# Expert loop of an attention and mixture-of-experts kernel: the second bias of odd tiles added in PSUM, GpSimd's additions one iteration later, the routing operations in the even tiles

## The reference, cut to what matters

```python
x = x + xattn(layernorm(x), ctx_768, ...)     # 8192 tokens of 512, 16 heads, FFN 1024
# then the mixture of experts, one expert per token:
logits = xt @ Wg.T;  top1 = argmax(logits)    # 8 experts
xhat = (xt - mean) * rsqrt(var + 1e-5)
for e in range(8):                            # H = 128
    h = gelu((xhat * s_e + b_e) @ w1_e + b1_e)
    y = y + (top1 == e) * (h @ w2_e + b2_e)
x = x + y
```

## Time and profile before

| | |
|---|---|
| median of 3 runs | 1581.79 us (1581.66 to 1583.35) |
| the profiled execution | 1584.45 us, span in the trace 1582.6 us |
| PE busy | 1515.4 us, 96% |
| DVE busy | 1037.9 us, 66% |
| POOL busy | 441.9 us, 28% |
| expert loop in the trace | first product of B_Y at 1402.79 us, last tile's L1506 at 1577.9 us |

### The profile page before, as it was taken

One profiled execution on the slowest core, in us unless ns is written; L12 is line 12 of the kernel. 1 busy time (PEld: TensorE's weight loads), 2 busy tenths in 40 slices (PEclk: granted clock), 3 DMA queues, 4 the chain that ended last, 5 costly groups with the idle time before them and its releaser, 6 DMA issues.

```text
span 1582.6 us, 24339 instructions
## 1 busy us (share of the span) xinstructions
PE 1515.4 (96%) x7988; PEld 1254.6 (79%) x7988; DVE 1037.9 (66%) x2496; ACT 713.1 (45%) x2015; POOL 441.9 (28%) x312
## 2 busy tenths in 40 slices
PE   6799999999999999999999999999999999997998
PEld 3688788787878787878787788878787878776886
DVE  5756566675758576766666675757575757467776
ACT  2545445353535363635444353535353636333443
POOL 3422122121222222212131122122222222136776
PEclk8899999999999999999999999999999999999999
DMA  9200101112020202020101101010101011548773
GB/s 230 80 28 1 54 1 40 42 31 74 3 86 1 74 14 74 22 75 21 61 27 54 34 23 38 17 54 1 54 1 54 1 54 54 215 153 261 232 226 112
DMA packets 67736, 105.93 MB, mean 67 GB/s; under 512 B 26967, under 2 KB 35432, under 8 KB 66591
## 3 DMA queue, kind: packets, MB, share of 16 engines
q1 hardware_dynamic: 56814, 70.68, 15.9%
q0 software_dynamic: 10800, 33.70, 5.5%
HBM read 59.47 MB, written 46.72 MB: 67 GB/s over the span
## 4 chain that ended last, share of the span: by engine, by line
PE 60%; DVE 23%; DMA 7%; ACT 4%; issue 3%; POOL 2%; DVEq 0%; POOLq 0%; SPq 0%; ACTq 0%
PE bank L1025 13%; PE bank L1050 12%; PE bank L887 11%; PE bank L911 5%; PE bank L1005 5%; DMA region<-rows,pos 4%; DVE actH L994 4%; PE bank L1455 4%; PE bank L1499 4%; DMA rows<-in_x 3%; DVE xn L845 2%; POOL region L1193 2%; ACT actH L988 2%; PE bank L1119 2%; PE bank L1438 2%
## 5 line engine op out<-in xcount | busy, mean ns | idle before, releaser
L1050 PE MATMUL bank<-w,actH 128*128 128x512 f32 x1536 | 373.8, 393 | 4.6 <-DVE actH L1040 4.6
L1025 PE MATMUL bank<-actA,w 128*128 128x512 f32 x1536 | 366.7, 394 | 0.0
L1025 PEld LDWEIGHTS bank<-actA,w 128*128 128x128 f32 x1536 | 286.0, 188 | 62.2
L1050 PEld LDWEIGHTS bank<-w,actH 128*128 128x128 f32 x1536 | 282.4, 188 | 62.9 <-DVE actH L1040 8.6
L970 POOL TENSOR_TENSOR E<-E,rc 128x1232 f32<-128x1232 f32 x64 | 145.0, 2265 | 447.6 <-DVE rc L965 447.6
L1040 DVE TENSOR_TENSOR actH<-htmp,actH 128x512 fp32r<-128x512 f32 x128 | 88.7, 693 | 166.8 <-ACT actH L1036 148.1
L1035 ACT ACTIVATE htmp<-bank,b 128x512 f32<-128x512 f32 x128 | 88.2, 689 | 226.1 <-PE bank L1025 217.4
L887 PE MATMUL bank<-actA,wq 128*128 128x512 f32 x768 | 182.0, 390 | 0.0
L943 ACT ACTIVATE E<-bank,mx 128x77 f32<-128x77 f32 x512 | 157.6, 365 | 45.4 <-DVE mx L920 45.4
L887 PEld LDWEIGHTS bank<-actA,wq 128*128 128x128 f32 x768 | 144.2, 188 | 30.4 <-issue 0.5
L1193 POOL DMA_INDIRECT region<-rows,pos x64 | 63.1, 985 | 373.0 <-DVE pos L1187 333.9
(11 more groups left out here) (165 smaller groups left out, 2063.3 us busy)
## 6 DMA issues: line engine op xcount, KB each, us to landing
rowB<-region SPq DMA_DIRECT2D x71, 258.0 KB
rows<-in_x SPq DMA_DIRECT2D x64, 256.0 KB, 3.5
e_raw<-in_E SPq DMA_DIRECT2D x16, 256.0 KB, 2.7
region<-padrow SPq DMA_DIRECT2D x9, 258.0 KB, 2.6
w_raw<-in_W SPq DMA_DIRECT2D x1, 2048.0 KB, 10.3
w_raw<-in_W SPq DMA_DIRECT2D x2, 1024.0 KB, 8.5
e_parts<-e_high SPq DMA_DIRECT2D x8, 256.0 KB, 2.0
e_parts<-e_low SPq DMA_DIRECT2D x8, 256.0 KB, 2.3
```

Of the source, the lines that this page charges most:

```text
L1025: mm = pe.matmul(p[:], w, a, start=k == 0 and j == 0, stop=k == KD - 1 and j == 2)
L1050: mm = pe.matmul(p[:], a, w, start=m == 0 and j == 0, stop=m == MF - 1 and j == 2)
```

## The change

Four edits, all in the expert loop:

1. Odd tiles: DVE no longer adds b2 to the row in SBUF. In B_Y(t) it adds b2 to the product in PSUM (`p = p + b2`, one input and the output in PSUM), then does L1488(t+1), and in a new step B_ROW(t) adds PSUM and row as before (`dve_bout`). Even tiles keep POOL's addition and one operation in B_Y.
2. POOL's addition of an even tile is in a step of its own, B_B2, three tiles ahead and not four: it stands in odd iterations, behind the scatter of an odd tile.
3. The drips of the loop move to even iterations: two after B_ROW and one after B_H, so three in two iterations in place of four.
4. SCAT of block 15 moves from iteration 6 to 14, TABLE2 from 8 to 5, PAD(e) from 10 + 2e to 16 + 2e. Registers: NREG 4 to 8.

```diff
-                3: [("RK", NBLK - 1)], 5: [("COUNT", 1)], 6: [("SCAT", NBLK - 1)], 8: [("TABLE2",)]}
-        LATE.update({10 + 2 * e: [("PAD", e)] for e in range(NE)})
+                3: [("RK", NBLK - 1)], 5: [("COUNT", 1), ("TABLE2",)], 14: [("SCAT", NBLK - 1)]}
+        LATE.update({16 + 2 * e: [("PAD", e)] for e in range(NE)})
         for t in range(-5, NT):
-            for kind, ahead in (("B_Y", 0), ("B_G", 1), ("B_X", 5), ("B_XT", 4), ("B_H", 3)):
+
+            for kind, ahead in (("B_Y", 0), ("B_G", 1), ("B_ROW", 0), ("B_X", 5), ("B_B2", 3), ("B_XT", 4), ("B_H", 3)):
                 if 0 <= t + ahead < NT:
                     step(kind, t + ahead)
+                if kind in ("B_ROW", "B_H") and t % 2 == 0:
+                    step("DRIP", 2 if kind == "B_ROW" else 1)
...
-        DRIP = {"KP": 5, "Q": 2, "PT": 2, "AV": 2, "HLO": 12, "Y": 1, "TT": 1, "B_Y": 1, "B_H": 1}
+        DRIP = {"KP": 5, "Q": 2, "PT": 2, "AV": 2, "HLO": 12, "Y": 1, "TT": 1}
...
-        NREG = 4
+        NREG = 8
...
-        def add_b2(eng, who, t):
-
-            eng.wait_ge(S["b_xT"], t + 1)
-            if t < 2:
-                eng.wait_ge(L["eb"], 32)
+        def pool_b2(pool, t):
+
+            if t % 2:
+                return
+            pool.wait_ge(S["b_xT"], t + 1)
+            if t == 0:
+                pool.wait_ge(L["eb"], 32)
             r = rowB[t % NROW][:, 0:D]
-            eng.tensor_tensor(r, r, pick(b2e, expert(eng, who, t)), ALU.add).then_inc(b_xb[t % 2], 1)
-
-        def pool_bx(pool, t):
-            if t % 2 == 0:
-                add_b2(pool, "pool", t)
-
-        def dve_b2(dve, t):
-            if t % 2:
-                add_b2(dve, "dve", t)
+            nc.gpsimd.tensor_tensor(r, r, pick(b2e, expert(pool, "pool", t)), ALU.add).then_inc(S["b_rb"], 1)
...
         def dve_by(dve, t):
             dve.wait_ge(S["b_y"], t + 1)
-            dve.wait_ge(b_xb[t % 2], t // 2 + 1)
+            p = of("B_Y", t)
+            if t % 2:
+                dve.tensor_tensor(p[:], p[:], pick(b2e, expert(dve, "dve", t)), ALU.add).then_inc(S["b_pb"], 1)
+            else:
+                dve.wait_ge(S["b_rb"], t // 2 + 1)
+                dve_bout(dve, t)
+
+        def dve_brow(dve, t):
+            if t % 2:
+                dve.wait_ge(S["b_pb"], t // 2 + 1)
+                dve_bout(dve, t)
+
+        def dve_bout(dve, t):
             r = rowB[t % NROW][:, 0:D]
             dve.tensor_tensor(r, of("B_Y", t)[:], r, ALU.add).then_inc(S["b_out"], 1)
...
-            "B_XT": {"pe": pe_bx, "act": act_bx, "dve": dve_b2, "pool": pool_bx},
+            "B_XT": {"pe": pe_bx, "act": act_bx},
+            "B_B2": {"pool": pool_b2},
+            "B_ROW": {"dve": dve_brow},
```

More of the change, by code:

```diff
@@ L264, in xattn_moe_kernel @@
             "pe_cnt dve_cnt dve_pad dve_tab dve_e1a pe_e1 dve_e1 act_e2 dve_e2 "
-            "b_xT b_xTs b_h b_hb b_gl b_g b_ghi b_glo b_y b_out").split()}
+            "b_xT b_xTs b_h b_hb b_gl b_g b_ghi b_glo b_y b_rb b_pb b_out").split()}
         pe_k, pe_v = S["pe_k"], S["pe_v"]
-        b_xb = [sem("b_xb0"), sem("b_xb1")]
         sched = []
```

## The result

The changed kernel takes 1588.23 us (median of 6 runs, 1587.24 to 1591.57) against 1581.72 us (1580.41 to 1583.35) in the same series: ratio 1.0044, interval 1.0031 to 1.0056. It is 6.5 us slower; 9.4 us faster was forecast. The profiled execution took 1587.24 us, its span is 1585.4 us. A second profiled run of each (e1, e12) gives 1583.7 and 1586.9.

What follows compares the result with a forecast made beforehand. PE was taken to nearly bound tiles 21 to 69, with more lost before. Terms of -5.0 (tiles 21 to 69), -4.7 (5 to 21) and +0.3 (0 to 5) sum to -9.4: 1581.8 to 1572.4 us, range 1566 to 1580.

Steps and rivals of the forecast that it cites:

- Part 4: Tiles 5 to 21: scatters at 14; together with Part 3 the loss falls from 12.7 to 8.0 us, -4.7 us.
- the stop: Iterations 9 to 11: L1466's unexplained 2.91 us wait, counted as gone; might return at SCAT for about 3.5 us.
- Rival (b): Expert loop: the stop returns at SCAT, or drips stall in iterations 16 to 20 too; 1576 us, chance 0.18.
- three signs of being wrong: Profile after: PSUM addition longer than 0.72 us, steady pairs waiting on POOL's L1424, or no stretched drips.
- Part 3: Even iterations 6 to 14: the first drip stalls at POOL's addition, 1.0 us a pair, 5.0 us in all.
- Tiles 0 to 5: Start of the expert loop: one more row-statistics stall, +1.0, less 0.7 us from DVE's emptier queue: +0.3 us.
- forecast wait of L1506(18) for POOL: Tile 18, behind the scatters: L1506 waits 2.4 us for POOL's addition, and PE waits behind it.
- Part 1: Tiles 21 to 69: PSUM addition takes 0.69 us, even tiles are on time, 0.21 us in 24 pairs: -5.0 us.
- rival (e): Odd tiles: the PSUM addition is long, 3.5 us per 0.1 us beyond 0.72, up to 1590 us; chance 0.08.
- Part 2: POOL's queue: 4.05 us of work fits a pair's 4.30; the addition keeps 1.7 us of slack, before 4.8.
- rival (d): Even tiles wait for POOL, whose pair takes 4.51 us; the 5.0 us gain goes, 1577.4 to 1580 us; chance 0.11.
- Rival (c): Drips: only one starting inside POOL's addition waits, 2.25 us in place of 5.0; 1569.6 or 1568 us; chance 0.13.

Runs made afterwards that it cites:

- e1: The kernel before, unchanged, once more for a second trace: a single execution of 1585.53 us beside a median of 1584.86 us in its series.
- e12: The kernel after, unchanged, once more: 1589.51 us, 1.0045 of the kernel before.
- e8: The kernel after with its three drips behind `hb` of odd tiles in place of even ones: 1583.64 us, 1.0019 of the kernel before.
- e15: The kernel after with the four scatters back in iteration 6, PAD and TABLE2 as after: 1.0028 of the kernel before.
- e17: The kernel before with only the LATE table of after (scatters at 14, TABLE2 at 5, PAD from 16 on): 1.0015 of the kernel before.
- e5: The kernel after with SCAT, TABLE2 and PAD where they were before: 1589.1 us, 1.0027 of the kernel before.
- e7: The kernel after without POOL's additions and the wait for them, even tiles going without b2: 1573.21 us, 0.9945 of the kernel before.
- e10: The kernel before with three drips behind L1488 of even tiles in place of two in every tile: 1580.38 us, 0.9984 of the kernel before.
- e4: The kernel after with before's drips, one after B_Y and one after B_H in every iteration: 1591.56 us, 1.0046 of the kernel before.
- e6: The kernel before with block 15's four scatters one at a time in iterations 6, 8, 10 and 12: 1581.11 us, 0.9996 of the kernel before.
- e9: The kernel after with drips in odd tiles and block 15's scatters one at a time in 9, 11, 13, 15: 1582.13 us, 1.0005 of before.
- e11: The kernel before with three drips behind L1488 of even tiles and scatters one at a time in 6, 8, 10, 12: 1577.34 us, 0.9968 of before.
- e16: The kernel after with drips in odd tiles, single scatters in 9, 11, 13, 15, TABLE2 at 8, PAD from 10 on: 1.0014 of before.
- e2: The kernel before with the addition of b2 in PSUM for odd tiles alone, before's order kept, NREG 8: 1588.17 us, 1.0022 of before.
- e14: The kernel after with the PAD steps at 10 + 2e as before, all else as after: 1.0035 of the kernel before.

## Why the prediction was wrong, step by step

**What failed.** The forecast said 1572.4 us and gave slower 0.07. Its sum had three terms, -5.0, -4.7 and +0.3, and each came out 2.4 to 5.3 us worse in the trace, beside a fourth that was not in it. Two causes make up most of it. Part 4 was counted as taking the stop away, and the stop only moved (2.7 us more than the term had there), while the drain grew by 2.6 us. And routing operations stalled at POOL's addition in more places, and held PE for longer, than was counted: 2.2 us in iterations 6 to 14, 1.3 in iteration 20, 2.4 in tiles 0 to 5. The rest is 1.9 us in the odd tiles. Rival (b) named both main causes, as one or the other, for 3.5 us. None of the three signs of being wrong came, as none of them watched the stop or the end of the program.

**Part 3 (first drip meets POOL's addition): the mechanism right, the size and the count not.** The drips of iterations 6 to 14 stalled, all five, as forecast; they took 1.2 to 1.7 us each. The pairs paid 0.8, 1.3, 1.3, 1.8 and 1.9 us, 7.2 together in place of 5.0. The term of 1.0 took `hb` to follow the drip at once; it does so 0.3 to 1.1 us later, "issue" in the row at 1437.26, while DVE's queue loads the register of the expert (L1380), 0.30 us in iterations 6 to 10, 0.84 and 0.92 us in 12 and 14, where the pairs paid most. In a tile on time this load lies in DVE's idle time. Iterations 18 and 20, called free because POOL would have no addition beside them, stalled too (1.60 and 1.64 us), and so did the row statistics in 2 and 4.

**Tiles 0 to 5: mis-sized.** The term was +0.3 with one stall; there were two, 1.93 and 1.81 us, and tiles 3 and 5 came after 4.41 and 4.38 us in place of 2.93 and 2.61, tile 4 after 2.43 in place of 3.05: +2.7. The term took the 1.0 us of part 3 once, less 0.7 us that was read from no row.

**Part 4 (scatters at 14): the step that failed.** It counted the stop of iterations 9 to 11 as gone, and put its return only in rival (b). Nothing in the change took its cause away. It came back behind the burst and cost (5.99 - 2.15) + (3.46 - 2.15) = 5.1 us, the lower clock behind it included. The forecast wait of L1506(18) for POOL, 2.4 us, isn't there in the row at 1460.28: the addition of tile 18 ended at 1457.16, 12.3 us after the product of tile 14 as forecast (12.9), but the stop had held the tile longer. Whether the wait would be there without the stop is not shown: in e8 a stalled drip stands in its place. So tiles 5 to 21 lose 7.2 + 5.1 + 1.0 = 13.3 us, where 8.0 were forecast and 12.7 stood before.

**The closing drain: not in the sum at all.** Part 4 adds 2.6 us behind the last tile (e15, e17), and the medians fit it: 1.0015 with part 4 alone (e17), 0.0017 less without it (e5). Before's trace held the row of 3.23 us; the prediction priced everything up to the last scatter, and nothing told that its end could depend on a place 50 tiles earlier.

**Part 1 (addition in PSUM): the duration right, the gain eaten elsewhere.** Forecast 0.69 us, measured 0.70, none above 0.72 behind tile 21; rival (e) is out. The even tile is on time and 0.20 us are won in each of 24 pairs, 4.8 us. But the odd tile starts 0.10 us late through the register operation and costs 0.08 in as many pairs, 1.9 us; one stalled pair costs 1.3. That leaves 1.6 of the 1.7 us measured. The slack "+2.9 before +3.15" was right, and not what mattered: the path of 2.17 us through DVE had no slack, as rival (e) says itself. The estimate from the Trainium skill (Perfetto Trace Analysis, "Optimizing Scalar/DVE Operations"), 0.755 us, is not borne out by the 0.70 us. The 1.2 us that it would have cost are not there; the 1.9 us lost in the odd tiles come from the later start.

**Part 2 (POOL's addition later): right on POOL, wrong in what it brings near.** In the steady pairs POOL never set the pace, so rival (d) is out. But the addition now follows the even iteration's drips; e7 without additions is 0.9945, e8 with the drips moved away 1.0019, e10 with before's additions and drips moved 0.9984. The stalls are shown by removal and by displacement on both sides.

**Rival (c).** A drip started up to 0.6 us ahead of POOL's recorded addition (0.7 in before) waits for its end, so the reading that whoever issues first holds the ports (Trainium skill, SBUF — State Buffer, "Who interferes with whom") does not fit the recorded starts, here as before. That the two exclude each other fits.

**What stays open.** What holds DVE until 7.4 to 9.0 us after a burst of four scatters begins, in eleven of the traces (in e4 it is DVE and ACT, until 5.8 us). The burst is needed (e6, e9, e11 and e16 have no stop). It alone is not enough: e7, without additions, has the burst and no stop, and so has the one trace of e8. Open are also why the closing drain depends on the place of the scatters, and what makes PE's semaphores late in e2. Parts 2 and 3 have no run of their own. The single effects of parts 1 and 4 (e2 1.0022, e17 1.0015) happen to add up to 1.0037 of 1.0044, but that is no account of the loss: the lateness that made e2 slow is not in the traces of the kernel after, which has the stalls instead.

## What to carry to other kernels

Small VectorE operations that are let out between the big ones are not free by their size. Put them where no GpSimd elementwise operation runs or starts within the next microsecond; moved so in the kernel before, they gave 0.9984, and with the burst of scatters spread 0.9968. A stop that no row explains must be counted as staying until an edit is known to take its cause away. When work is moved in a queue, look at the end of the program as well.

## What the runs showed of the hardware that was not expected

- A 0.15 us DVE operation on few elements (128x1, 128x8, 1x18), started 0.15 to 0.7 us before the recorded start of an elementwise operation of POOL that follows an indirect transfer, takes 1.5 to 2.1 us in most cases, until POOL's operation ends; beside the indirect transfer alone (e7) it takes 0.15. Over all traces none of some 380 that started 0.7 to 3 us ahead took over 0.4 us.
- A DVE addition with both the source and the destination in PSUM, 128x512 fp32, takes 0.70 us; with the row in SBUF as second source and destination it takes 0.69.
- POOL's closing drain is 3.0 to 3.3 or 5.9 us, by the place of four indirect transfers more than 100 us earlier.
- Behind four back-to-back indirect transfers (0.96 us each) DVE waits 2.9 to 5.9 us in eleven traces, and goes on 7.4 to 9.0 us after the first of them started; PE runs behind it at 1.2 GHz for a while in ten of them (not in e14).
